# Graph layer on one core: one-hots laid out node by node, compared as 16-bit numbers

## The reference, cut to what matters

```python
xn = layernorm(x)                      # x: 6250 nodes x 256
m = (xn @ W + b)[src]                  # 100000 edges, sorted by dst
h = segment_sum(m, dst, 6250) / max(degree, 1)
x = x + h + linear_attention(xn)       # 8 heads
x = x + experts(layernorm(x))          # best of 8 experts, at most 977 rows each
```

## Time and profile before

| | |
|---|---|
| median of 3 runs (lowest, highest) | 1551.4 us (1550.78, 1553.32) |
| the profiled execution: its own time | 1551.53 us |
| the profiled execution: span, first to last instruction | 1549.8 us |
| busy in the span: PE (TensorE matmuls) / PEld (weight loads) | 1124.6 / 762.9 us |
| busy in the span: DVE (VectorE) / ACT (ScalarE) / POOL | 906.8 / 513.5 / 918.1 us |
| mean granted TensorE clock | 0.875 |

### The profile page before, as it was taken

One profiled execution on the slowest core, in us unless ns is written; L12 is line 12 of the kernel. 1 busy time (PEld: TensorE's weight loads), 2 busy tenths in 40 slices (PEclk: granted clock), 3 DMA queues, 4 the chain that ended last, 5 costly groups with the idle time before them and its releaser, 6 DMA issues.

```text
span 1549.8 us, 33330 instructions
## 1 busy us (share of the span) xinstructions
PE 1124.6 (73%) x5569; PEld 762.9 (49%) x5570; DVE 906.8 (59%) x3297; ACT 513.5 (33%) x1355; POOL 918.1 (59%) x966
## 2 busy tenths in 40 slices
PE   2669886445444565787888778887888888887996
PEld 2346553112222233555656556555555555555895
DVE  5854433133333454676667777777777777777564
ACT  2832221011111132343434434444444334444242
POOL 4546777777766776777677766666474456511111
PEclk9999997566666678899999999999899999999898
DMA  7493333444444455455455555555454445423462
GB/s 234 152 261 102 104 104 112 127 133 136 134 132 126 133 167 163 143 177 169 147 174 170 177 159 168 156 153 172 145 173 146 149 150 165 145 94 109 134 191 92
DMA packets 143360, 231.62 MB, mean 149 GB/s; under 512 B 29824, under 2 KB 87329, under 8 KB 143248
## 3 DMA queue, kind: packets, MB, share of 16 engines
q0 software_dynamic: 42896, 115.65, 25.1%
q1 hardware_dynamic: 99118, 114.27, 23.4%
q10 hardware_dynamic: 1234, 0.66, 0.2%
HBM read 197.40 MB, written 35.08 MB: 150 GB/s over the span
## 4 chain that ended last, share of the span: by engine, by line
DVE 29%; issue 27%; POOL 16%; PE 11%; DVEq 9%; ACT 2%; DMA 2%; POOLq 2%; SPq 1%; ACTq 0%
POOL shared L570 16%; DVE shared L1346 4%; PE pY L964 3%; PE pH L973 2%; PE pA L875 2%; DVEq L1301 2%; DVEq L1296 2%; PE pH L855 2%; DVE shared L1466 1%; DVE shared L1464 1%; DMA shared<-table,idx 1%; DVE shared L1455 1%; DVE shared L1469 1%; DVE stats L1387 1%; DVE shared L1463 1%
## 5 line engine op out<-in xcount | busy, mean ns | idle before, releaser
L570 POOL DMA_INDIRECT shared<-table,idx x784 | 765.2, 976 | 312.8 <-issue 274.8
L875 PE MATMUL pA<-shared,onehot 128*128 x976 | 341.5, 470 | 263.2 <-POOLq L550 165.3
L875 PEld LDWEIGHTS pA<-shared,onehot 128*128 x976 | 100.4, 103 | 488.8 <-issue 419.1
L1288 DVE TENSOR_TENSOR onehot<-tile_iota,dst_t 128x512 f32 x244 | 159.8, 695 | 156.3 <-PE pA L875 117.3
L964 PE MATMUL pY<-w2s,shared 128*128 x864 | 203.6, 390 | 5.8 <-issue 4.6
L973 PEld LDWEIGHTS pH<-shared 128*128 128x128 f32 x1728 | 201.4, 192 | 2.7
L973 PE MATMUL pH<-shared 128*128 128x128 f32 x1728 | 201.7, 275 | 0.0
L680 ACT ACTIVATE shared<-pA,rdeg 128x256 f32<-128x256 f32 x49 | 23.2, 473 | 473.3 <-DVE rdeg L1358 473.3
L964 PEld LDWEIGHTS pY<-w2s,shared 128*128 128x128 f32 x864 | 164.0, 195 | 30.0 <-issue 7.3
L730 ACT ACTIVATE shared<-pH,b1s 128x128 f32<-128x128 f32 x432 | 119.8, 376 | 107.9 <-PE pH L973 89.5
L523 POOL DMA_INDIRECT rows<-rows_sb,row_at x49 | 51.6, 1054 | 159.4 <-issue 159.4
(11 more groups left out here) (254 smaller groups left out, 1585.4 us busy)
## 6 DMA issues: line engine op xcount, KB each, us to landing
shared<-in_L_ffn_w_dram SPq DMA_DIRECT2D x108, 512.0 KB, 4.6
shared<-table,idx POOLq DMA_INDIRECT x784
w2s<-in_L_ffn_w_dram SPq DMA_DIRECT2D x8, 1024.0 KB, 6.3
rows<-rows_sb SPq DMA_DIRECT2D x7, 1040.0 KB, 14.7
shared<-rows SPq DMA_DIRECT2D x54, 130.0 KB
shared<-in_L_ffn_b_dram SPq DMA_DIRECT2D x54, 128.0 KB
shared<-in_x_dram SPq DMA_DIRECT2D x12, 512.0 KB, 8.7
table<-w2s SPq DMA_DIRECT2D x12, 512.0 KB, 3.2
```

What stands on the lines that cost most here:

```text
L570: g.indirect_dma_start(gathered[:, s * G + j, :], None, table[:, :], bass.IndirectOffsetOnAxis(ap=idx[:, q * G + j:q * G + j + 1], axis=0) ...
L875: m = pe.matmul(pA[:, :], onehot[:, n % OQ, j, :], gathered[:, (f % RQ) * G + j, :], start=False, stop=final and j == G - 1)
L1288: v.tensor_tensor(onehot[:, n % OQ, :, :], tile_iota[:, :].rearrange("p (a n) -> p a n", a=1).broadcast_to([P, G, P]), dst_t[:, bass.ds(ch ...
```

## The change

A one-hot's layout turns from chunk by chunk (four blocks of 128 nodes) to node by node (128 nodes with the group's four edges side by side). Its two inputs become f16: `node_no` holds each of the numbers 0 to 127 four times and stays as it is, and `dst_r` holds the destinations relative to the tile. So `next_tile` no longer adds 128 to 128 numbers but subtracts `tile_at[t + 1]` (128 times the tile) from all 784 columns of `dst_t`, f32 in and f16 out. TensorE's weights for chunk j are then every fourth number of the slot. The padding's destination is 30000 instead of 100000. Source numbers are kept as uint16. `iota_i` lies in the new `node_no`.

```diff
@@ -68,7 +68,7 @@
 GW = D + NX
 BIG = 1.0e6
 EPS = 1e-5
-PAD_DST = 100000.0
+PAD_DST = 30000.0
 MAGIC = 1.5 * 2.0 ** 23
 
 
@@ -176,7 +176,7 @@
         eps = sb("eps", [P, 2])
 
 
-        src_t = sb("src_t", [P, ECP], I32)
+        src_t = sb("src_t", [P, ECP], mybir.dt.uint16)
         dst_t = sb("dst_t", [P, ECP])
         cmin = sb("cmin", [P, EBLK])
         cmax = sb("cmax", [P, EBLK])
@@ -192,12 +192,14 @@
         planw = sb("planw", [1, PB * 2], I32)
         ends = sb("ends", [1, 3, NT], I32)
         idx = sb("idx", [P, IDX], I32)
-        onehot = sb("onehot", [P, OQ, G, P], F16)
+        onehot = sb("onehot", [P, OQ, P, G], F16)
         sel_f = onehot[:, :, :, :].rearrange("p a b c -> p (a b c)").bitcast(F32)
-        tile_iota = sb("tile_iota", [P, P])
+        dst_r = sb("dst_r", [P, ECP], F16)
+        node_no = sb("node_no", [P, P, G], F16)
+        tile_at = sb("tile_at", [P, NT])
         mv = sel_f[:, 0:2 * NT].rearrange("p (t a) -> p t a", a=2)
         rstd = sel_f[:, 2 * NT:3 * NT]
-        iota_i = tile_iota[:, :].bitcast(I32)
+        iota_i = node_no[:, :, :].rearrange("p n g -> p (n g)").bitcast(I32)[:, 0:P]
 
         stats = sb("stats", [P, 2, NB, 6])
 
@@ -872,7 +874,7 @@
                     pe.sem_inc(S["pe_hold"], 1)
                     pe.wait_ge(S["oh_ready"], n + 1)
                     for j in range(G):
-                        m = pe.matmul(pA[:, :], onehot[:, n % OQ, j, :], gathered[:, (f % RQ) * G + j, :], start=False,
+                        m = pe.matmul(pA[:, :], onehot[:, n % OQ, :, j], gathered[:, (f % RQ) * G + j, :], start=False,
                                       stop=final and j == G - 1)
                         if j == 0:
                             m.then_inc(S["oh_slots"], 1)
@@ -1259,7 +1261,9 @@
             c.mark(v.scalar_tensor_tensor(ends[0:1, 1, :], new_row[0:1, 0:NT], float(EARLY), lh_row[0:1, 0, 0:NT], ALU.min, ALU.add))
             c(v.tensor_scalar(rounds, base_row[0:1, NT - 1:NT], 1.0 / BODY, float(TURNS), ALU.mult, ALU.add))
             v.sem_inc(S["spans_ok"], 1)
-            c.mark(v.tensor_copy(tile_iota[:, :], iota_row[:, :]))
+            c.mark(v.tensor_copy(node_no[:, :, :], iota_row[:, :].rearrange("p (n a) -> p n a", a=1).broadcast_to([P, P, G])))
+            c.mark(v.tensor_copy(dst_r[:, :], dst_t[:, :]))
+            c.mark(v.tensor_scalar(tile_at[:, :], iota_row[:, 0:NT], float(P), None, ALU.mult))
             c(v.tensor_copy(tok[:, :], chunk_id[:, 0:1]))
 
             def keys(t, b):
@@ -1285,9 +1289,8 @@
                     n = v.snap(pair_r)
                     if wait:
                         v.wait_ge(S["oh_slots"], n)
-                    v.tensor_tensor(onehot[:, n % OQ, :, :],
-                                    tile_iota[:, :].rearrange("p (a n) -> p a n", a=1).broadcast_to([P, G, P]),
-                                    dst_t[:, bass.ds(ch % EQ * G, G)].rearrange("p (g a) -> p g a", a=1).broadcast_to([P, G, P]),
+                    v.tensor_tensor(onehot[:, n % OQ, :, :], node_no[:, :, :],
+                                    dst_r[:, bass.ds(ch % EQ * G, G)].rearrange("p (a g) -> p a g", a=1).broadcast_to([P, P, G]),
                                     ALU.is_equal).then_inc(S["oh_ready"], 1)
                     v.reg_add(pair_r, pair_r, 1)
 
@@ -1325,7 +1328,7 @@
                     v.wait_ge(S["oh_ready"], v.snap(pair_r))
                     v.sem_inc(S["dve_hold"], 1)
                     p = part("tile_c", t)
-                    p(v.tensor_scalar(tile_iota[:, :], tile_iota[:, :], float(P), None, ALU.add))
+                    p(v.tensor_scalar(dst_r[:, :], dst_t[:, :], tile_at[:, bass.ds(t + 1, 1)], None, ALU.subtract))
                     early()
 
                 def queries(t):
```

## The result

The changed kernel takes 1563.1 us (median of four runs, 1560.9 to 1564.1) against 1551.1 us for the kernel before on the same chip: 1.0074 times as long, with a 95% interval of 1.0057 to 1.0092. The profiled execution took 1563.57 us, its span is 1561.8 us.

A forecast was written before the change was run, and what follows sets the result against it. Bound by POOL's gathers from 125 to 640 us, then VectorE's chain for 38 steps. Setup +0.5, POOL stage -3.5 + 1.0, VectorE stage +17.5 - 1.3 make +14.2 us: 1565.6 us, range 1554 to 1583.

The forecast's parts named there:

- The early one-hots gain nothing: Loop of 3 or 4 one-hots per step: sequencer sets the 0.61 us lap, so shorter comparisons gain only some 0.04 us.
- rival 1: One-hot loop: the lap falls with the comparison, 0.27 us for each of some 136 one-hots, -21 us, 1530 us; 10%.
- The rebase: VectorE, once per tile: 0.63 us, 0.40 more than now, plus 0.10 for the scalar's column; +17.5 us over 38 steps.
- Late fifth one-hots: Five tiles behind the POOL stage: a fifth group's one-hot is wholly on the path, 0.27 us less each, 1.3 us gained.
- POOL stage: Gathers on POOL, 125 to 640 us: shorter one-hots hold up fewer gathers, -3.5 us; rebases hold some up, +1.0 us.
- Rebase against gathers: Tiles 0 to 9: rebases delay POOL's gathers by chance hits, 0.1 us a tile, 1 us in all.
- Setup: At 92 us, ahead of the first one-hots: three operations replace one on VectorE, +0.5 us (0 to 1.2).
- Weights: TensorE's weight loads at steps of 8 bytes could double from 0.1 us, hidden behind the lap; taken as nothing.
- rival 4: TensorE becomes the bound through slow strided weights, loads of 0.38 us: +34 on the sum, 1600 us; 5%.
- Rival 2: VectorE's rebase runs at the slow pace, near 1 us: +31 us, 1583 us; 14%.
- rival 3: One-hots on VectorE: the comparison does not get shorter, as its second operand repeats four numbers: +21 us, 1572 us; 10%.
- rival 5: Gathers cover more of the 38 steps and the POOL stage may gain its full 5 us: 0 to +8, 1555 us; 11%.

The follow-up runs named there:

- experiment 2: The changed kernel with its 16-bit one-hots laid out chunk by chunk again, the rebase kept: 1569.0 us, 1.0096 of before.
- experiment 3: The changed kernel with node-by-node one-hots compared as f32, destinations rebased in place by subtracting 128: 1566.4 us, 1.0091 of before.
- second execution of before: The kernel before run once more, unaltered: 1554.6 us in its one run.
- second pair: The kernel before and the changed kernel, each profiled once more, unaltered: 1554.6 us and 1564.9 us.
- experiment 4: The changed kernel with its rebase issued ahead of the register load and waited for behind it: 1536.9 us, 0.9892 of before.
- experiment 1: The changed kernel with its rebase cut to 128 of the 784 columns, most one-hots wrong: 1542.9 us, 0.9932 of before.
- experiment 10: The changed kernel with 16-bit integers rebased in place, the rebase left behind the register load: 1552.8 us, 1.0001 of before.

## Why the prediction was right, and where it was not

*The early one-hots gain nothing.* Right. The lap is 0.61 us with comparisons of 0.70 and of 0.43 us; rival 1 is excluded by experiment 2, and so is the rule of the Trainium skill (VectorE: DVE Perf Modes, "The perf-mode tier table") as a forecast of time. The rate itself is borne out in node order, where 512 elements take 0.43 us, as long as 256 in f32; in chunk order, where one operand repeats each number 128 times, two 16-bit operands ran at the f32 pace, 0.70 us. The 0.04 us behind the last one-hot came too: 2.24 against 2.19 in the table. The first loop, with laps of 0.84 in the earlier trace rows, ran at 0.61 after the change:

```profile
97.74 0.43 DVE L1292 TENSOR_TENSOR onehot<-node_no,dst_r 128x512 f16 x1 [0.19 <-issue]
98.36 0.42 DVE L1292 TENSOR_TENSOR onehot<-node_no,dst_r 128x512 f16 x1 [0.19 <-issue]
98.96 0.42 DVE L1292 TENSOR_TENSOR onehot<-node_no,dst_r 128x512 f16 x1 [0.18 <-issue]
```

That isn't the comparison's doing: experiments 2 and 3, with comparisons of 0.70 us, ran it at 0.61 too, and the second execution of before at 0.84 again, as did experiment 5, which is the kernel before with its add moved. It goes with the program, not with the operation, which is what a lap of the sequencer would do.

*The rebase.* Right in mechanism and close in size: 0.63 us forecast and measured, so 0.40 more than the add; 0.08 for the column, where I had 0.10. By these medians a step should lose 0.48 - 0.05 = 0.43 us; from the reciprocal of step 17 to that of step 47, in the two first profiles, it loses 12.0 us over 30 steps, 0.40 each. The rest is in the operations that a gather held up, which a median leaves out: in the means of these steps the add takes 0.27 us and the rebase 0.65, the way from the degrees to the first one-hot grows by 0.46, and 0.46 - 0.05 = 0.41. I also counted one rebase too many: the last step has no next tile, so the 38 steps have 37. With 1.3 us for the late one-hots, 37 x 0.41 - 1.3 = 13.9 us; the 38 steps lost 13.7, where my terms gave 16.2.

*Late fifth one-hots.* Right as a mechanism. In the chain at the tile of the earlier trace rows:

```profile
646.33 0.44 DVE onehot L1292
...
647.10 1.16 PE pA L877 x4
```

From the one-hot's start to TensorE's sums it is now 0.77 us, 1.07 before.

*POOL stage.* This is the term that failed. I had tile 10's sums some 2 us earlier; they came at 624.7 us before and 625.0 after (625.7 and 625.9 in the second pair). The gathers did get shorter, by 2.6 of my 3.5 us. What I left out is that POOL doesn't only issue gathers there: before each scatter it waits until it has reported the group before as landed, and those eight pauses took 3.7 us more. The pauses are 7.4 and 7.6 us with the add or the integer rebase moved, 9.6 with the integer rebase left in place, 10.5 with the f16 rebase moved, 11.0 to 12.1 in experiments 1 to 3: by and large they are longer where VectorE has more to do ahead of its one-hots, but experiment 4 doesn't fit that, each is one execution, and why the landing is reported later was not settled. Tiles 0 to 9 do have the cover that I claimed for the rebase, but it isn't whole.

*Rebase against gathers.* I took 1 us by a rate of chance hits. In the changed kernel there were hardly any: six of the eleven rebases up to 640 us began 0.5 to 0.7 us after a gather, and only one in the first execution and two in the second held a gather up. VectorE's operations are released by sums, and those by gathers; I take it that this puts them at a fixed distance from the gathers, where my rate had them at random. What I overlooked is that the gather then holds the rebase. Those six took 0.65 to 0.82 us, the longer the earlier they began in the gather. The longest began 0.52 us into one:

```profile
440.43 0.96 POOL L572 DMA_INDIRECT shared<-table,idx  x1 [0.16 <-issue]
...
440.95 0.82 DVE L1331 TENSOR_SCALAR dst_r<-dst_t,tile_at 128x784 f16<-128x784 f32 x1 [1.02 <-issue]
```

*Setup.* The three operations cost what was forecast (0.43, 0.56 and 0.18 us), but as the first loop's laps were shorter this time, the keys began no later. *Weights:* a load takes 117 ns, 14 more than before, behind TensorE's lap; rival 4 needed 0.25 us a load, and is excluded by experiments 1, 2 and 10. *Source numbers in 16 bits:* nothing seen.

*Other rivals and the sums.* Rival 2 falls with the rebase's 0.63 us, rival 3 with the one-hot's 0.43, and rival 5 with the 13.7 us that the 38 steps lost. Two slips in the prediction's sums change no conclusion: its upper end is +37 (34 + 2 + 1.2), not +36, and rival 5, from 0 to +8, holds no time that is faster by more than 3.1 us.

The mechanism of the loss was right, but that the sum came within some 2 us was partly luck: the POOL stage with the setup was 2.7 us too low and the steps 2.5 us too high, with 2 us of the tail on top that two executions can't assign.

## What to carry to other kernels

Ask of a short operation in a loop what its lap is made of: if the sequencer sets the lap, a faster operation only buys idle time, and anything added ahead of the loop on the same engine's path costs in full. Where an engine's sequencer is held by a register load, an operation that it can start beforehand is free, and the load itself can go under the engine's longest operation; here the two moves were worth some 40 us together, the comparison's own speed a few at most. And a change judged slower may be worth keeping once what it added is covered.

## What the runs showed of the hardware

- Two 16-bit operands made the comparison of 512 elements shorter (0.43 us against 0.70) only in the order in which the repeated operand is four numbers side by side. Repeating one number 128 times left it at 0.70.
- A gather that starts while a rebase runs is held until the rebase is done. Of experiment 4 (rebases of 0.63 us), experiment 3 (0.57) and experiment 10 (0.37), each rebase with its gather:

```profile
259.13 0.63 DVE L1330 TENSOR_SCALAR dst_r<-dst_t,tile_at 128x784 f16<-128x784 f32 x1 [0.42 <-issue]
259.26 1.32 POOL L572 DMA_INDIRECT shared<-table,idx  x1 [0.31 <-issue]
...
314.96 0.63 DVE L1330 TENSOR_SCALAR dst_r<-dst_t,tile_at 128x784 f16<-128x784 f32 x1
...
315.15 1.25 POOL L572 DMA_INDIRECT shared<-table,idx  x1 [0.30 <-issue]
```

```profile
595.71 0.57 DVE L1329 TENSOR_SCALAR dst_t<-dst_t 128x784 f32<-128x784 f32 x1 [1.17 <-issue]
595.87 1.26 POOL L571 DMA_INDIRECT shared<-table,idx  x1 [1.76 <-issue]
```

```profile
593.19 0.37 DVE L1331 TENSOR_SCALAR dst_r<-dst_r 128x784 int16<-128x784 int16 x1 [1.20 <-issue]
...
593.31 1.09 POOL L572 DMA_INDIRECT shared<-table,idx  x1 [1.77 <-issue]
```

  All four gathers end 0.81 to 0.85 us after the rebase's end, whatever its length and their own start; undisturbed they take 0.95. So the hold ends with the rebase, and some 0.1 us of a gather's work (an estimate: 0.95 less 0.81 to 0.85) goes on beside it. A gather begun 0.02 us into a rebase (at 805.81 us in experiment 4) was not held. By the Trainium skill (SBUF — State Buffer, "SBUF: two separate sides") the engine that has the shared port pair keeps it for its whole instruction. The trace agrees for the rebase, at 0.37, 0.57 and 0.63 us.
- The hold goes the other way too. In the changed kernel a rebase that began 0.50 to 0.69 us into a gather was stretched to as much as 0.87 us, and ended as if it had begun 0.71 to 0.74 us after the gather's start; one that began 0.02 to 0.44 us into a gather, or 0.86 us and later, took its usual 0.63.
- A rebase of 784 numbers took 0.63 us from f32 to f16 with a scalar per partition, 0.57 in f32 in place with a constant, and 0.365 in 16-bit integers in place.
- Weights read at steps of 8 bytes load in 117 ns in place of 103.
